# Cross-attention and expert layer on one core: a pair's 52 slots in 26 groups of two, VectorE's additions behind each group's second maxima, denominators in four column tiles

## The reference, cut to what matters

```python
def attention(x, context, Wq, Wk, Wv, Wo, bo):        # x: 2048 tokens x 256, context: 1601 x 192
    q = heads(x @ Wq); k = heads(context @ Wk); v = heads(context @ Wv)     # 16 heads of 64
    scores = q @ k.T / sqrt(64)
    return softmax(scores) @ v @ Wo + bo
x = x + attention(layernorm(x), context, ...)
x = x + experts(layernorm(x), ...)                    # 8 experts, top tokens of each
```

## Time and profile before

| | |
|---|---|
| median of three runs | 1381.43 us |
| the profiled execution | 1375.65 us |
| its span | 1373.9 us |
| PE busy | 1296.3 us, 94% |
| DVE busy | 1023.0 us, 74% |
| POOL busy | 906.8 us, 66% |
| ACT busy | 798.8 us, 58% |
| granted TensorE clock, mean | 0.971 of full |

### The profile page before, as it was taken

The page is one execution under the profiler, slowest core; times in us unless marked ns, Lnnn a source line. Parts: engine busy times, 40 slices in busy tenths (PEclk is TensorE's granted clock), DMA queues, the critical chain, the costliest instruction groups (busy, mean ns, idle before and its releaser), DMA issues. The chain is left out here.

```text
span 1373.9 us, 24841 instructions
## 1 busy us (share of the span) xinstructions
PE 1296.3 (94%) x8308; PEld 819.1 (60%) x8308; DVE 1023.0 (74%) x1708; ACT 798.8 (58%) x1061; POOL 906.8 (66%) x464
## 2 busy tenths in 40 slices
PE   7989999999999999999999999999999926999996
PEld 5655555555555555554555555555447915999996
DVE  5867877887787788778778877887977775666662
ACT  5456666666665666566566666656664213657753
POOL 3347877887787688779777877977687002445553
PEclk9999999999999999999999999999999956999998
DMA  9530010002001100200010010002313442545422
GB/s 275 201 111 9 25 42 31 17 20 62 17 25 39 37 17 16 65 17 17 26 57 16 17 57 25 17 17 77 128 39 123 160 151 60 146 130 126 106 37 28
DMA packets 76631, 88.83 MB, mean 65 GB/s; under 512 B 11579, under 2 KB 56412, under 8 KB 76508
## 3 DMA queue, kind: packets, MB, share of 16 engines
q1 hardware_dynamic: 69724, 78.32, 17.5%
q0 software_dynamic: 6784, 8.94, 4.0%
HBM read 58.98 MB, written 27.99 MB: 63 GB/s over the span
## 5 line engine op out<-in xcount | busy, mean ns | idle before, releaser
L915 POOL TENSOR_TENSOR acc_p<-acc_p,x_in 128x1024 f32<-128x1024 f32 x192 | 488.0, 2542 | 135.5 <-ACT x_in L1012 128.7
L112 DVE TENSOR_REDUCE mx_part<-ps_m 128x1 f32<-128x512 f32 x552 | 363.0, 685 | 173.5 <-PE ps_m L81 172.7
L1012 ACT ACTIVATE x_in<-ps_s 128x1024 f32<-128x1024 f32 x384 | 380.6, 1024 | 100.7 <-PE ps_s L831 71.3
L843 PE MATMUL ps_o<-x_in,v 128*64 128x512 f32 x1664 | 406.2, 606 | 0.0
L820 PE MATMUL ps_s<-q,k 64*128 64x512 f32 x2496 | 386.4, 396 | 1.2 <-ACT x_in L1012 1.2
L820 PEld LDWEIGHTS ps_s<-q,k 64*128 64x128 f32 x2496 | 273.8, 185 | 41.5 <-ACT x_in L1012 7.8
L81 PE MATMUL ps_m<-k,q 64*128 64x512 f32 x736 | 215.6, 456 | 9.8 <-PEq L228 3.8
L843 PEld LDWEIGHTS ps_o<-x_in,v 128*64 128x64 f32 x1664 | 99.5, 136 | 180.7 <-issue 140.7
L81 PEld LDWEIGHTS ps_m<-k,q 64*128 64x128 f32 x736 | 100.9, 184 | 168.3 <-issue 112.5
L915 DVE TENSOR_TENSOR acc_d<-acc_d,x_in 128x1024 f32<-128x1024 f32 x96 | 166.4, 1733 | 5.2 <-ACT x_in L1012 4.9
L697 ACT ACTIVATE kept<-ps_m 128x512 f32<-128x512 f32 x184 | 109.7, 596 | 83.0 <-PE ps_m L81 82.9
(11 more groups left out here) (251 smaller groups left out, 1936.3 us busy)
## 6 DMA issues: line engine op xcount, KB each, us to landing
w_in<-in_w SPq DMA_DIRECT2D x16, 1024.0 KB, 5.7
v_st<-rec_scr SPq DMA_DIRECT2D x64, 128.0 KB, 2.9
o_scr<-v_st SPq DMA_DIRECT2D x32, 256.0 KB, 2.1
v<-v_scr SPq DMA_DIRECT2D x8, 832.0 KB, 5.2
v_scr<-c_in SPq DMA_DIRECT2D x10, 512.0 KB, 3.9
c<-o_scr SPq DMA_DIRECT2D x2, 1792.0 KB, 8.0
x_in<-in_x SPq DMA_DIRECT2D x4, 512.0 KB, 9.8
m_rows<-mx_t SPq DMA_DIRECT2D x128, 1.0 KB
```

Of the source, the lines that this page charges most:

```text
L112: dve.tensor_reduce(part[:, j // S.MF, j % S.MF:j % S.MF + 1], bank[:, 0:S.MC], AX.X, ALU.max).then_inc(done or G.rough_used[hd], 1)
L843: last = pe.matmul(ps_o[hd * HP:hd * HP + DH, :], v[b][:, s, hd * DH:(hd + 1) * DH], probs[:, g % RING, hd * QC:(hd + 1) * QC], start=(s = ...
L915: eng.tensor_tensor(acc, other, probs[:, (u * KT + t) % RING, :], ALU.add).then_inc(done, 1)
L1012: act.activation(probs[:, g % RING, :], ps_s[:, g % 2, :], ACT.Exp, bias=G.pad_bias[:, 0:1] if s == KT - 1 else 0.0, scale=SCALE).then_inc ...
```

## The change

Groups are now pairs of consecutive slots over the whole pair: (0, 1), (2, 3), ... (50, 51). Since a unit has 13 slots, the groups of units 0 and 2 (called even below) are (0, 1) to (10, 11), then (12, slot 0 of the next unit); those of units 1 and 3 (odd) are (1, 2) to (11, 12). There are 26 instead of 28. In the group that straddles two units PE does the value products of three slots, and one in the next.

The first job of every group now has its head 1 copied by ACT (`KEPT` is gone): 26 a pair instead of 24. The counts that semaphores are compared with are worked out from the slot's number in place of tables.

DVE's additions move: in odd units tiles 3, 7 and 11 behind the maxima of slots 4, 8 and 12, in even units behind those of slots 3, 7 and 11; the last tile, 12, behind those of slot 1 of the next unit after an odd unit, and of slot 0 after an even one. Each is then behind the second maxima of a group. A projection is at slots 1 and 7 of even units and 2 and 8 of odd ones; DVE's part of it stands behind the maxima of slots 2 and 9, and 3 and 9. Of these only slot 9 of the even units is the second of its group.

The denominator is at slot 3 of even units and slot 4 of odd ones. It is made by four matmuls of 32 columns by 256 in place of two of 64 by 512, so that `den_sb` is half as wide and one DMA moves it.

```diff
-KEPT = (0, 2, 5, 7, 9, 11)
+DEN_TILES = 4
-GROUPS = ((0,), (1, 2), (3, 4), (5, 6), (7, 8), (9, 10), (11, 12))
-PROJ_PLACES = tuple((u, s) for u in range(UNITS) for s in (2, 8))
+PROJ_PLACES = tuple((u, s) for u in range(UNITS) for s in ((1, 7), (2, 8))[u % 2])
+DEN_PLACES = tuple((u, (3, 4)[u % 2]) for u in range(UNITS))
...
             pe.wait_ge(joined, unit + 1)
-            for b in range(2):
-                last = pe.matmul((ps_x if bank is None else bank)[b * HP:(b + 1) * HP, :], G.ones[:, 0:HP], acc_p[:, u % 2, b * QC:(b + 1) * QC],
-                                 start=True, stop=True)
+            for i in range(DEN_TILES):
+                last = pe.matmul((ps_x if bank is None else bank)[i * DP:(i + 1) * DP, 0:DQ], G.ones[:, 0:DP],
+                                 acc_p[:, u % 2, i * DQ:(i + 1) * DQ], start=True, stop=True)
...
-            for u in range(UNITS):
-                for n, group in enumerate(GROUPS):
-                    rough(u, group[0])
-                    for s in group:
-                        scores(u, s, then_rough=(s != group[0]))
-                    for s in GROUPS[n - 1]:
-                        values(u if n else u - 1, s)
-                    small(u, group[-1])
+            for g in range(0, SLOTS, 2):
+                rough(*divmod(g, KT))
+                for i in range(2):
+                    scores(*divmod(g + i, KT), then_rough=(i == 1))
+                joins_before, joins_here = (g - 2) % KT == KT - 1, g % KT == KT - 1
+                for n in range(g - 1 if joins_before else g - 2, g + 1 if joins_here else g):
+                    values(n)
+                for i in range(2):
+                    small(*divmod(g + i, KT))
...
-                if s == DVE_TILES[1] + 1:
-                    add_tile(dve, 0, u, unit, slot - s, dve=True)
                 if job:
...
-                if s == 0 and not (first and u == 0):
-                    add_tile(dve, ND - 1, (u - 1) % UNITS, unit - 1, slot - KT, dve=True)
-                if s - 1 in DVE_TILES[2:] and not (last and u == UNITS - 1 and s - 1 == DVE_TILES[-2]):
-                    add_tile(dve, DVE_TILES.index(s - 1) - 1, u, unit, slot - s, dve=True)
-                if divmod(g - 1, KT) in PROJ_PLACES and proj_here(PROJ_PLACES.index(divmod(g - 1, KT)), first, last):
-                    n = PROJ_PLACES.index(divmod(g - 1, KT))
-                    dve_proj(dve, n, 1 - b, proj_count(p, n), p)
+                late = u % 2
+                if s == 1 - late and not (first and u == 0):
+                    add_tile(dve, ND - 1, (u - 1) % UNITS, unit - 1, p * SLOTS + (u - 1) * KT, dve=True)
+                if s - late in DVE_TILES[1:-1] and not (last and u == UNITS - 1 and s - late == DVE_TILES[-2]):
+                    add_tile(dve, DVE_TILES.index(s - late) - 1, u, unit, slot - s, dve=True)
+                for n, at in enumerate(PROJ_PLACES):
+                    if at[0] == u and s == at[1] + (2 if at[1] == 7 else 1) and proj_here(n, first, last):
+                        dve_proj(dve, n, 1 - b, proj_count(p, n), p)
```

More of the change, by code:

```diff
@@ L663, in x_wait @@
             first = isinstance(p, int) and p == 0
-            users = [((a, DEN_SLOT), den_copied, UNITS * p + a) for a in range(1 if first else 0, UNITS)]
+            users = [(at, den_copied, UNITS * p + at[0]) for at in DEN_PLACES[1 if first else 0:]]
             users += [(at, stage_lo, proj_count(p, n) + 1) for n, at in enumerate(PROJ_PLACES) if proj_here(n, first, last)]
@@ L671, in x_wait, with jobs, kept_jobs, job_cols @@
                 pe.wait_ge(copied, count)
[L674 to L680, removed]
+        def jobs(p, g, head):
+            return MJOBS + MAHEAD + (p * SLOTS + g if head == 0 else p * GROUPS + g // 2)
+        def kept_jobs(p, g):
+            return p * GROUPS + (g + 1) // 2
+        def job_cols(j):
+            return S.MC if j < MJOBS - 1 else S.QT * S.MT
+        def pe_rough(pe, b, c, j, p, g, heads=(0, 1)):
             for hd in heads:
-                if hd and (j - 1) % MJOBS in KEPT:
-                    pe.wait_ge(kept_made, kept_count((j - 1) % MJOBS, unit if j else unit - 1) + 1)
+                if hd and g % 2:
+                    pe.wait_ge(kept_made, kept_jobs(p, g))
                 else:
-                    wait_for(pe, rough_used[hd], used_count(unit, j, hd))
+                    pe.wait_ge(rough_used[hd], jobs(p, g, hd))
                 rough_scores(S, G, pe, ps_m[:, hd, :], b, hd, c, j)
[L688 to L699, removed]
+        def act_rough(act, j, p, g):
+            n = job_cols(j)
+            wait_for(act, kept_read, kept_jobs(p, g) - 1)
+            act.wait_ge(rough_ready[1], jobs(p, g, 0) + 1)
+            act.activation(kept[:, g // 2 % 2, 0:n], ps_m[:, 1, 0:n], ACT.Copy).then_inc(kept_made, 1)
+        def dve_rough(dve, j, unit, p, g):
             if j == 0:
@@ L952, in scores, with values @@
                     pe_minus_max(pe, g, u, s, p * UNITS + u)
-            def values(u, s):
-                unit, g = p * UNITS + u, u * KT + s
+            def values(g):
+                u, s = divmod(g, KT)
+                unit = p * UNITS + u
                 if u >= 0:
@@ L962, in small @@
                 unit = p * UNITS + u
-                if s == DEN_SLOT and not (first and u == 0):
+                if (u, s) in DEN_PLACES and not (first and u == 0):
                     x_wait(pe, p, u, s, last)
@@ L1032, in rough @@
                     j, ahead = job
-                    act_rough(act, j, p * UNITS + u + ahead, (p * UNITS + u + ahead) * MJOBS + j)
-            for u in range(UNITS):
-                for group in GROUPS:
-                    rough(u, group[0])
-                    for s in group:
-                        exponentials(u, s)
-                    copies(u, group[-1])
-                    if last and (u, group[-1]) in WO_HI:
-                        pairs = wo_pairs(WO_HI.index((u, group[-1])))
+                    act_rough(act, j, p, u * KT + s)
+            for g in range(0, SLOTS, 2):
+                rough(*divmod(g, KT))
+                for i in range(2):
+                    exponentials(*divmod(g + i, KT))
+                for u, s in (divmod(g, KT), divmod(g + 1, KT)):
+                    copies(u, s)
+                    if last and (u, s) in WO_HI:
+                        pairs = wo_pairs(WO_HI.index((u, s)))
                         act.wait_ge(wo_loaded, 16)
                         act.activation(G.wo_hi[:, pairs, :], wo_in[:, pairs, :], ACT.Copy).then_inc(wo_hi_done, 1)
-                    if last and (u, group[-1]) in AHEAD_HI:
-                        act_ahead(act, AHEAD_HI.index((u, group[-1])))
+                    if last and (u, s) in AHEAD_HI:
+                        act_ahead(act, AHEAD_HI.index((u, s)))
         def dve_pair(dve, p, b, first=False, last=False):
```

40 lines of the change are left out of this document (20 added, 20 removed).

## The result

The changed kernel takes 1388.34 us in the median of six runs (1387.33 to 1389.85); the kernel before, timed with it, 1381.40. The ratio is 1.0044, with a 95% interval of 1.0033 to 1.0055: 6.1 us slower (the two medians alone differ by 6.9). The forecast was slower by 26 us, 1408. The way is right, the size is four times too large, and the time is that of rival C, 1387.7.

What follows compares the result with a forecast made beforehand. PE's own work was taken as the path, with DVE kept just in time. -5.6 - 8.1 + 40 = +26.4 us on the profiled 1375.65 gave 1402.1, in the runs' terms 1408; range 1363 to 1424.

Steps and rivals of the forecast that it cites:

- rival C: Only the odd units' tile 3 costs, the tenths in other places fall well: +6.3 us, 1387.7; chance 0.14.
- 16 groups fewer: Two groups fewer a pair, each costing PE 0.35 us for going in and out of two array shapes: -5.6 us.
- stall of the earlier trace gone: The 0.37 us a pair lost where a late maximum delayed the second rough matmul goes: -2.6 us.
- tile 11 behind unit 1: At the end of unit 1 DVE's late addition delays the next group's maximum, 0.5 us a pair: +3.5 us.
- denominators, 31: Each denominator costs 0.60 us instead of 0.86, with four column tiles abreast: -8.1 us, bounds -13 and +5.
- tile 3 in odd units: In group (3, 4) DVE's addition waits for POOL's tile 4; PE stalls 1.53 us, 15 times: +23.0 us.
- unit 0, tiles 7 and 11: In unit 0 both DVE additions wait for POOL's, delaying PE by 0.6 and 1.45 us a pair: +16.4 us.
- the collision in the odd units: In group (3, 4) DVE's addition, 0.43 us behind POOL's start, waits until 543.55 and ends at 544.64; stall 1.53 us.
- step 3: What DVE's moved additions meet: they wait for POOL's and stall PE, 5.2 us a full pair, +40 us.
- Unit 0, tile 7: Behind slot 7, POOL does tiles 4, 5, 6 in a row; DVE's addition ends at T6+6.9, stall 0.6 us.
- the prediction's own rule: Additions of DVE and POOL exclude each other; whoever comes first has it.
- rival B: DVE comes first in the odd units' group (3, 4), even units' places likewise: -16.7 us, 1364.7; chance 0.23.

Runs made afterwards that it cites:

- pool_second_wide: pool_second with the old denominators (two matmuls of 64 columns by 512): 1369.84 us, ratio 0.9961 to the kernel before.
- pool_second: The changed kernel, with POOL waiting in units 1 and 3 for DVE's tile 3 before adding tile 4: 1369.55 us, ratio 0.9885 to the kernel before.
- proj_half: The changed kernel, with DVE's projection part at slot 3 of odd units subtracting 256 of 512 columns: 1363.33 us, ratio 0.9907 to the kernel before.
- pause_u0: The changed kernel with a 128x128 memset on DVE ahead of tile 7's addition in unit 0: 1381.67 us, ratio 1.0051 to the kernel before.

## Why the prediction was wrong in size

| term | forecast | measured |
|---|---|---|
| 16 groups fewer | -5.6 | -5.4 together with the next two lines (pool_second_wide) |
| stall of the earlier trace rows gone | -2.6 | as above |
| tile 11 behind unit 1 | +3.5 | +2.4 (7 times 0.34 at the second matmul) to +3.2 (0.46 at the values) |
| denominators, 31 | -8.1 | -9.0 (31 times 0.29); 10.5 between pool_second_wide and pool_second |
| tile 3 in odd units | +23.0 (15 times 1.53) | +22.1 (14 times 1.58); pool_second without it 22 less |
| unit 0, tiles 7 and 11 | +16.4 | 0 |
| sum | +26.4 (the lines add up to 26.6) | +7.7 by these lines and in the traces' attentions, +6.1 by the ratio |

What bounds the kernel, the price of a group, the denominators with four tiles abreast, and the collision in the odd units with its two ends and its 1.5 us were right, to some tenths of a microsecond each. That the number is close to rival C's is no merit of the forecast: it gave C 0.14.

The step that failed is in step 3, "Unit 0, tile 7": "DVE comes at T6+3.2 at the earliest and ends at T6+6.9". It took POOL to be ahead of DVE there. With T6 = 458.77 (the group's first maximum starts at 459.31, 0.54 in) POOL's row of tile 6 begins at T6+3.45, DVE came at T6+3.60, and DVE went first, ending at T6+4.75: no stall, where 0.6 and 1.45 us a pair were in the sum, 16.4 us in all.

Three things were wrong in that step. First, it broke the prediction's own rule: by its numbers POOL's third addition begins at T6+3.4, so a DVE that comes at T6+3.2 is ahead of it, goes next and ends at T6+4.5. It wrote T6+6.9 as if POOL, with three additions in a row, kept its turn. Second, it left out the reciprocal, which stands between slot 7's maxima and the addition; in every place where POOL came ahead by 0.02 to 0.31 and DVE still went first, it was there. What exactly let DVE go first stays open, as said above; that it did, and that the stalls come back when it doesn't, is shown. Third, it set no margin beside this place, as it did for the odd units (0.43; in the kernel 0.27, since each of DVE's rows begins some 0.08 before the one ahead of it ends, and the sum laid the last ones end to end). Two terms a pair hung on that one sign, and the second only on the first. A place decided by less than the accuracy of the sum belongs among the rivals, not in the sum: then the forecast would have been rival C.

What rival B said, that the point is who comes first, was borne out by pool_second and proj_half; its condition just wasn't met.

## What to carry to other kernels

Where two engines exclude each other, look at who is issued first and by how much, and let a semaphore decide it if one of them has slack: here a wait on the engine with slack turned 0.4% slower into 1.15% faster. A cut on the busy engine pays only where nothing stood just behind its cover: the same cut of the denominators was worth nothing in the old order and 10 us once the stalls were gone. And in a forecast, give each term that hangs on a tenth of a microsecond a chance of its own.

## What the runs showed of the hardware that was not expected

- Beside a reciprocal, POOL's row may begin first and DVE still goes first. With a 16x64 reciprocal less than a microsecond ahead of DVE's addition, DVE was first in 90 places of the traces, at lags up to 0.31 us (pause_u0), and POOL in 64. Without one DVE was first at no lag above 0.01, be POOL idle before (proj_half: first at 0.01, not at 0.03) or not. Whether it is the reciprocal, or in part that POOL's addition stood behind another of its own, was not tried apart.
- The one that waits, waits for the whole of the other's instruction: DVE ends 1.08 or 1.09 us behind the end of POOL's addition in each case shown.
- Four column tiles of 32 run abreast on fp32 data of their own: eight instructions of 256 columns in 0.57 us with the change of the array's shape, against 0.86 for four of 512.
